# A ternary product turned first: two token tiles of a convolution moved from TensorE to ScalarE and VectorE

## The reference, cut to what matters

```python
h = bit_linear(x, w1)                 # x quantised per token, w1 ternary: 128 -> 512
h = depthwise_conv1d(h.transpose(0, 2, 1), conv_w, conv_b)   # 3 taps over tokens, padding 1
h = jax.nn.silu(h.transpose(0, 2, 1))
return bit_linear(h, w2)              # h quantised per token, w2 ternary: 512 -> 128
```

## Time and profile before

| what | value |
|---|---|
| median of 3 runs | 322.48 us (315.58 to 322.57) |
| the profiled execution | 317.07 us |
| its span, first to last instruction | 314.2 us |
| mean granted TensorE clock | 0.989 of full |

### The profile page before, as it was taken

One profiled execution on the slowest core, in us unless ns is written; L12 is line 12 of the kernel. 1 busy time (PEld: TensorE's weight loads), 2 busy tenths in 40 slices (PEclk: granted clock), 3 DMA queues, 4 the chain that ended last, 5 costly groups with the idle time before them and its releaser, 6 DMA issues.

```text
span 314.2 us, 6619 instructions
## 1 busy us (share of the span) xinstructions
PE 283.5 (90%) x2446; PEld 179.3 (57%) x2446; DVE 219.8 (70%) x481; ACT 195.1 (62%) x484; POOL 143.1 (46%) x252
## 2 busy tenths in 40 slices
PE   0899699899999989989899999999999988898893
PEld 0567556566666668656566677445445443355672
DVE  3777767896776642869566747988888689527834
ACT  2588467668777760886677820778867866534333
POOL 3523767794477762565465500086326208001320
PEclk9999889999999999999999999999999999999997
DMA  7920000000000000000000000000000000000001
GB/s 273 306 87 3 0 3 1 2 2 0 3 2 3 2 0 2 0 3 0 2 2 3 2 2 0 2 0 0 2 0 3 1 0 3 0 2 0 8 17 42
DMA packets 4834, 6.16 MB, mean 20 GB/s; under 512 B 834, under 2 KB 3650, under 8 KB 4676
## 3 DMA queue, kind: packets, MB, share of 16 engines
q1 hardware_dynamic: 4516, 5.42, 4.9%
q10 hardware_dynamic: 288, 0.33, 0.4%
HBM read 5.23 MB, written 0.52 MB: 18 GB/s over the span
## 4 chain that ended last, share of the span: by engine, by line
PE 67%; DVE 19%; ACT 7%; issue 5%; DMA 1%; POOL 1%; ACTq 0%; DVEq 0%; POOLq 0%
PE bank L721 58%; PE bank L794 5%; ACT pr L545 4%; DVE nmax L1343 3%; DVE qk L1388 3%; DVE xn L1287 1%; DMA x_sb<-in_x 1%; ACT pT L545 1%; DVE stats L1274 1%; PE bank L946 1%; PE bank L848 1%; DVE qs L1323 1%; PE bank L1014 1%; DVE xn L1669 1%; DVE pT L1359 1%
## 5 line engine op out<-in xcount | busy, mean ns | idle before, releaser
L645 ACT ACTIVATE pT<-bank 128x512 f32<-128x512 f32 (+1 forms) x80 | 44.5, 600 | 25.6 <-PE bank L721 25.1
L338 POOL TENSOR_SCALAR pr<-pr,pinv 128x256 f32<-128x256 f32 (+2 forms) x96 | 45.5, 492 | 29.7 <-DVE pinv L1351 29.6
L1388 DVE TENSOR_REDUCE qk<-bank 128x4 fp32r<-128x616 f32 x64 | 49.0, 796 | 13.6 <-PE bank L721 13.4
L545 ACT ACTIVATE pr<-bank,nmax 128x256 f32<-128x256 f32 (+2 forms) x96 | 44.4, 480 | 18.2 <-DVE nmax L1343 17.9
L721 PE MATMUL bank<-qs 64*128 64x256 f32 (+3 forms) x256 | 50.4, 477 | 4.1 <-ACT pr L545 3.8
L1343 DVE TENSOR_REDUCE nmax<-bank 128x2 f32<-128x512 f32 (+2 forms) x48 | 31.6, 687 | 14.5 <-PE bank L721 14.5
L721 PE MATMUL bank<-pT,v_sb 128*64 128x128 f32 (+2 forms) x320 | 38.4, 385 | 0.0
L338 POOL TENSOR_SCALAR pT<-pT,pinv 128x512 f32<-128x512 f32 x32 | 21.8, 693 | 23.9 <-DVE pinv L1351 23.9
L1359 DVE COPY pT<-bank 128x512 f32<-128x512 f32 (+1 forms) x32 | 30.4, 949 | 1.6 <-PE bank L794 1.5
L721 PEld LDWEIGHTS bank<-pT,v_sb 128*64 128x64 f32 x320 | 21.1, 136 | 14.1 <-issue 10.8
L721 PE MATMUL bank<-km,qk 64*128 64x308 f32 x128 | 27.7, 366 | 1.2 <-DVE qk L1388 1.1
(11 more groups left out here) (190 smaller groups left out, 578.9 us busy)
## 6 DMA issues: line engine op xcount, KB each, us to landing
pT<-in_wqk SPq DMA_DIRECT2D x1, 1024.0 KB, 6.3
cw_sb<-in_cw SPq DMA_DIRECT2D x1, 768.0 KB, 8.8
x_sb<-in_x SPq DMA_DIRECT2D x2, 256.0 KB, 5.5
pT<-in_wv SPq DMA_DIRECT2D x1, 512.0 KB, 7.1
wo_sb<-in_wo SPq DMA_DIRECT2D x1, 512.0 KB, 7.3
out<-x_sb SPq DMA_DIRECT2D x8, 64.0 KB, 1.5
onT<-in_consts ACTq DMA_DIRECT2D x1, 256.0 KB, 5.0
pT<-in_xwk SPq DMA_DIRECT2D x1, 256.0 KB, 7.5
```

Of the source, the lines that this page charges most:

```text
L338: nc.gpsimd.tensor_scalar(d, d, pinv[:, t, a:a + 1], 1.0, ALU.mult, ALU.mult).then_inc(norm_done, 1)
L545: nc.scalar.activation(prob[r][:, a, at:at + w], bank[:, SP[k % 2] + a, at:at + w], ACT.Exp, bias=nmax[:, t, a:a + 1], accum_out=psum[:, t ...
L645: nc.scalar.activation(px[rows, i, :], bank[rows, (ST0, ST1)[i % 2], :], ACT.Exp, scale=SD ** -0.5).then_inc(xexp_done, 1)
L1388: nc.vector.tensor_reduce(m, s_in, AX.X, ALU.max, negate=True).then_inc(round_done, 1)
```

## The change

For tokens 256 to 511 of batch 1 (tiles 6 and 7) the product with ternary w1 is made with hidden units on partitions: for each of 4 blocks of 128 hidden units (`hidden_block`) two products of 258 columns (128 channels in, w1 exact in fp32r in `w1_t`, the tokens' high and low part) into banks 1 and 2 in turn. ScalarE makes the centre tap with the bias (`centre_tap`, 128 x 256), VectorE adds the two outer taps (`outer_taps`, two scalar_tensor_tensor of 128 x 256) into `tap_y`, which lies in `qs`. After all four blocks TensorE transposes them back into the banks of tiles 6 and 7 (`turn_taps`, four transposes each), in place of `conv(6)` and `conv(7)`. The weights of the taps, per hidden unit, come by one more load (`taps`, 16 values per partition), and w1 stays ternary without its mean: GpSimd multiplies the mean into the taps and, in three more passes, into the convolution rows in step 8; it also copies w1 to `w1_t` at the start of `bias_rows`. The down products use two banks in turn (`DOWN_BANK`), so each waits for the `finish` two tiles back. In the tail ScalarE does both last silus ahead of `turned_hidden` 4 to 7.

```diff
@@ -45,6 +45,9 @@
 HALF = NT // 2
+TAPPED = (1,)
+NB = FH // P
+TAP_BANK = (1, 2)
 KEY_BANK = (0, 5)
@@ -54,6 +57,7 @@
 HIDDEN_BANK = (ST0, ST1)
+DOWN_BANK = (OB, PJ0)
 OUT_BANK = (ST1, ST0)
@@ -79,7 +83,7 @@
 def decoder_layer(nc, x, consts, wqk, wv, wo, ctxT, xwq, xbq, xwk, xbk, xwv, xbv, xwo, xbo, lam_in,
-                  w1, cw, cb, w2, out):
+                  w1, cw, cb, w2, taps, out):
     with ExitStack() as ctx:
@@ -148,6 +152,7 @@
         wc = cw_sb
+        tap_sb = sb("tap_sb", [P, NB, 4])
         wsum = sb("wsum", [P, 2])
@@ -202,6 +207,8 @@
         qf = onT[:, 6:8, :]
+        tap_y, = places(qs[:, :, :].rearrange("p a b -> p (a b)"), (NB, T // 2))
+        w1_t = xT_l[:, 0, :]
         qb0, qb1, qa = qk[:, 0, 0, 0:2, :], qk[:, 0, 0, 2:4, :], qk[:, 0, 1, 0:2, :]
@@ -251,6 +258,7 @@
         root_done = sem("root_done")
+        tap_ps, tap_act, tap_done, tap_scaled = sem_names("tap_ps", "tap_act", "tap_done", "tap_scaled")
         pool_chain, qb0_pool, scale_done, hdq_done, hq_last = sem_names(
@@ -273,7 +281,7 @@
             sp.dma_start(wo_sb[:, :, :], wo).then_inc(ld_o, 16)
-            for dst, src in ((w1_sb[:, :], w1), (w2_sb.rearrange("p (k c) -> p k c", c=C), w2),
+            for dst, src in ((tap_sb[:, :, :], taps), (w1_sb[:, :], w1), (w2_sb.rearrange("p (k c) -> p k c", c=C), w2),
                              (cw_sb[:, :, :].rearrange("p a d -> p (a d)"), cw.to_broadcast([P, 3 * FH]))):
@@ -379,6 +387,12 @@
                     pool.wait_ge(w1d_done, 1)
+                    nc.gpsimd.tensor_scalar(tap_sb[:, :, 0:3], tap_sb[:, :, 0:3], wmean[:, 0:1], 1.0, ALU.mult,
+                                            ALU.mult).then_inc(tap_scaled, 1)
+                    for k in range(3):
+                        link(nc.gpsimd.tensor_scalar(cw_sb[:, k, :], cw_sb[:, k, :], wmean[:, 0:1], 1.0, ALU.mult,
+                                                     ALU.mult))
+                    settle()
                     for k in range(3):
@@ -452,6 +466,8 @@
+                pool.wait_ge(xq_ps, NG)
+                nc.gpsimd.tensor_copy(w1_t, w1_sb[:, :]).then_inc(tap_scaled, 1)
                 pool.wait_ge(ld_cb, 16)
@@ -676,6 +692,16 @@
+            def centre_tap(b, k):
+                v = NB * TAPPED.index(b) + k
+                act.wait_ge(tap_ps, v + 1)
+                if v == 0:
+                    act.wait_ge(tap_scaled, 1)
+                if v == NB:
+                    act.wait_ge(conv_ps, NT)
+                nc.scalar.activation(tap_y[:, k, :], bank[:, TAP_BANK[k % 2], 1:T // 2 + 1], ACT.Identity,
+                                     bias=tap_sb[:, k, 3:4], scale=tap_sb[:, k, 1:2]).then_inc(tap_act, 1)
             whole, halves = slice(0, T), (slice(0, T // 2), slice(T // 2, T))
@@ -709,11 +735,18 @@
             turned_hidden(1)
-            for i in range(4, TT):
-                silu(i)
-                turned_hidden(i - 2)
-            turned_hidden(TT - 2)
-            turned_hidden(TT - 1)
+            silu(4)
+            centre_tap(1, 0)
+            centre_tap(1, 1)
+            turned_hidden(2)
+            centre_tap(1, 2)
+            centre_tap(1, 3)
+            silu(5)
+            turned_hidden(3)
+            silu(TT - 2)
+            silu(TT - 1)
+            for i in range(TT - 4, TT):
+                turned_hidden(i)
@@ -998,6 +1031,32 @@
+            def hidden_block(b, k):
+                v = NB * TAPPED.index(b) + k
+                if k == 0:
+                    pe.wait_ge(xdTl_done, 1 if b == 0 else 3)
+                if v == 0:
+                    pe.wait_ge(tap_scaled, 2)
+                if k < 2 and b == 0:
+                    pe.wait_ge(round_done, part_sums + 2)
+                elif k < 2:
+                    pe.wait_ge(silu_done, 3 + k)
+                else:
+                    pe.wait_ge(tap_done, v - 1)
+                o, w = bank[:, TAP_BANK[k % 2], 0:T // 2 + 2], w1_t[:, P * k:P * k + P]
+                mm(o, w, xdT_h[:, b, T // 2:T + 2], True, False)
+                mm(o, w, xdT_l[:, b, T // 2:T + 2], False, True).then_inc(tap_ps, 1)
+            def turn_taps(i):
+                pe.wait_ge(tap_done, NB * TAPPED.index(i // NT) + NB)
+                at = P * (i % NT - HALF)
+                for k in range(NB):
+                    last = nc.tensor.transpose(bank[:, CONV_BANK[i % 4], P * k:P * k + P], tap_y[:, k, at:at + P],
+                                               con[:, C_ID:C_ID + P])
+                last.then_inc(conv_ps, 1)
             def turn_hidden(i):
@@ -1019,10 +1078,12 @@
                     pe.wait_ge(xo_done, 2)
+                elif i == 1:
+                    pe.wait_ge(xdTl_done, 3)
                 else:
-                    pe.wait_ge(f_done, i)
+                    pe.wait_ge(f_done, i - 1)
                 for k in range(FH // P):
-                    last = mm(bank[:, OB, 0:C], hiT[:, i % 2, k * P:k * P + P], w2_q[:, k, :], k == 0,
+                    last = mm(bank[:, DOWN_BANK[i % 2], 0:C], hiT[:, i % 2, k * P:k * P + P], w2_q[:, k, :], k == 0,
                               k == FH // P - 1)
@@ -1247,11 +1308,19 @@
             turn_hidden(1)
-            conv(5)
-            for i in range(6, TT):
-                down(i - 5)
-                turn_hidden(i - 4)
-                conv(i)
+            conv(5, [0])
+            hidden_block(1, 0)
+            hidden_block(1, 1)
+            conv(5, [1])
+            down(1)
+            turn_hidden(2)
+            hidden_block(1, 2)
+            hidden_block(1, 3)
+            conv(5, [2])
+            down(2)
+            turn_hidden(3)
+            turn_taps(6)
+            turn_taps(7)
             for i in range(TT - 4, TT):
@@ -1308,8 +1377,7 @@
                 if k == 0:
-                    nc.vector.tensor_scalar(w1_sb[:, :], wq1, -1.0, wmean[:, 0:1], ALU.max,
-                                            ALU.mult).then_inc(w1d_done, 1)
+                    nc.vector.tensor_scalar(w1_sb[:, :], wq1, -1.0, None, ALU.max).then_inc(w1d_done, 1)
                     dve.wait_ge(w1d_done, 1)
@@ -1420,7 +1488,7 @@
             row_max(0, 1)
-            dve.wait_ge(ld_f, 48)
+            dve.wait_ge(ld_f, 64)
             for k, w in enumerate((w1_sb, w2_sb)):
@@ -1621,6 +1689,18 @@
+            def outer_taps(b, k):
+                v = NB * TAPPED.index(b) + k
+                dve.wait_ge(tap_act, v + 1)
+                if v == 0:
+                    dve.wait_ge(tap_scaled, 1)
+                ps = bank[:, TAP_BANK[k % 2], :]
+                link(nc.vector.scalar_tensor_tensor(tap_y[:, k, :], ps[:, 0:T // 2], tap_sb[:, k, 0:1], tap_y[:, k, :],
+                                                    ALU.mult, ALU.add))
+                settle()
+                nc.vector.scalar_tensor_tensor(tap_y[:, k, :], ps[:, 2:T // 2 + 2], tap_sb[:, k, 2:3], tap_y[:, k, :],
+                                               ALU.mult, ALU.add).then_inc(tap_done, 1)
             def half_root(h):
@@ -1703,7 +1783,7 @@
                 dve.wait_ge(f_ps, i + 1)
-                nc.vector.scalar_tensor_tensor(x_sb[:, i, :], bank[:, OB, 0:C], hdq[:, i:i + 1],
+                nc.vector.scalar_tensor_tensor(x_sb[:, i, :], bank[:, DOWN_BANK[i % 2], 0:C], hdq[:, i:i + 1],
                                                x_sb[:, i, :], ALU.mult, ALU.add).then_inc(f_done, 1)
@@ -1716,7 +1796,15 @@
             hidden_scale(3)
-            for i in range(4, TT):
+            outer_taps(1, 0)
+            outer_taps(1, 1)
+            finish(0)
+            hidden_scale(4)
+            outer_taps(1, 2)
+            outer_taps(1, 3)
+            finish(1)
+            hidden_scale(5)
+            for i in range(6, TT):
                 finish(i - 4)
@@ -1750,7 +1838,7 @@
 _NAMES = ["x", "consts", "wqk", "wv", "wo", "ctxT", "xwq", "xbq", "xwk", "xbk", "xwv", "xbv", "xwo", "xbo",
-          "lam_in", "w1", "cw", "cb", "w2"]
+          "lam_in", "w1", "cw", "cb", "w2", "taps"]
@@ -1815,6 +1903,8 @@
         "cb": g["L0_ffn_conv_b"][None, :],
+        "taps": np.concatenate([g["L0_ffn_conv_w"][:, 0, :], g["L0_ffn_conv_b"][:, None]], 1).reshape(
+            FH // P, P, 4).transpose(1, 0, 2),
         "w2": g["L0_ffn_w2"].T.reshape(FH // P, P, C).transpose(1, 0, 2),
```

## The result

The changed kernel takes 320.49 us (median of four, 320.4 to 320.72). Ratio to the kernel before 1.0124, 95% interval 1.0086 to 1.0162. The profiled execution takes 320.45 with a span of 318.4, against 317.07 and 314.2: the sum for it had said 315.1, so it is off by 5.3 us, and in direction.

A forecast was written before the change was run, and what follows sets the result against it. TensorE, busy 283.5 of 314.2 us, was taken as the bound, with the end waiting on one tile's path. Tail gains of 1.2 + 0.8 + 0.4, less 0.4 for the clock, gave 322.48 - 2.0 = 320.5 us, range 312.9 to 323.0.

The forecast's parts named there:

- the copy in `bias_rows`: GpSimd copy of 0.6 us before the xd transposes: no direct cost, taken as 0, with -1.0 to +0.6 kept.
- The tail: End of batch 1, tiles 4 to 7: gain 1.2 + 0.8 + 0.4 = 2.4 us, 2.0 after the clock.
- The thinnest cover: In the tail, the silu of tile 7 ends near 305.9 and VectorE wants it at 306.1: 0.2 us.
- The clock in the tail: Half speed may come before the last transposes as TensorE's work thins: 0.4 us taken off, up to 1.0.
- The two down banks: Kernel's end: last transposes start 0.05 behind the quantise, gain 0.8 us; `down(7)` 0.05 behind ScalarE, gain 0.4.
- POOL at n = 8: GpSimd's scale and three tap products ahead of `normalise(9, 0)`: 2.4 us under 8.5 us of cover, cost 0.
- the load: One more DMA issue on SP ahead of w1, w2 and cw: adds some 0.5 us, hidden, cost 0.
- Nothing is left of the tail: Rival for the tail: gain under 0.7 us through thin cover, clock and port order, giving 322; chance 0.14.
- slower, because DVE becomes a dearer bound: Rival for the tail: eight scalar_tensor_tensor at 0.73 us break even; with early half clock 323.2; chance 0.10.
- PE stays the bound: Rival for the tail: VectorE's pairs hidden, TensorE's whole saving back, 2.4 plus up to 1.0 us, giving 319; chance 0.06.
- The level of the runs: Rival for the whole kernel: runs mostly at the lower level, median 313.6 to 315.1 whatever the change does; chance 0.25.

The follow-up runs named there:

- filling the wait: Changed kernel with eight unused products of 512 columns in TensorE's queue ahead of its wait for the xd tiles: 314.17 us, ratio to the kernel before 0.9922.
- the new order: Changed kernel with bias_rows (with its copy) ahead of inverse_root(0, 5) in GpSimd's list: 311.73 us, ratio to the kernel before 0.9853.

## Why the prediction was wrong, step by step

**The step that failed is the copy in `bias_rows`.** The prediction had the two ends, "DVE ends 0.6 later" or "up to 1.0 earlier", and took 0. The upper end came: the order of the two operations was kept, 267.02 before 267.06, and TensorE's start moved by 0.55 more than the 0.09 ahead of it. But the step stopped at the delay. It had TensorE's wait of 1.30 in the earlier trace rows and a paragraph on the clock, and never put the two together: the clock was looked for in the tail only, where the work is thinned, and not where a wait that existed already got longer. The half clock there is no term of the sum: 6.1 us by the shifts, 6.3 by filling the wait. The sign that was to warn, a wait other than 1.3 by more than 0.6, was set too wide as well: 0.55 more was enough. The Trainium skill, "TensorE: Matmul & The Clock Gate", section "What's actually happening", which was weighed for the tail, applied here too: after little activity the engine is left at half rate, and full rate comes back only after it has been busy. The trace agrees in the order of things: the clock falls at 270.2, behind a stretch in which PE was busy 2.15 of 4 us, and is back at 283.9 behind 13.7 us in which it was busy throughout. Why the return takes that long here and 6.8 us in another execution, no run shows.

**The median came out as forecast, 320.49 for 320.5, by two errors that met, which is luck.** 322.48 was the median of three executions, two of which were at the upper level. The prediction called the level a property of the runs, "whatever the change does". It was the half clock, which the changed kernel had in all four executions (mean granted clock 0.972 or 0.973 in each, 0.989 in the profile of before): 322.5 less the tail's 2.5 and plus the 0.55 of the longer wait gives 320.5. Against the lower level, which the ratio uses, the same kernel is 1.2% slower. With the term put right the sum for the profiled execution is 317.07 + 0.1 + 0.55 + 6.1 - 2.5 = 321.3, for 320.45 measured; by spans 314.2 + 4.2 = 318.4, as measured. The 0.9 between the two sums lies outside the span (2.9 us in the profiled execution of before, 2.0 in this one).

**The tail was right.** Forecast 2.4 before the clock; the shifts give 2.53: 1.21 up to the last quantise (1.2 forecast), 0.82 to the last transposes (0.8), 0.32 to `down(7)` (0.4), and 0.18 that the forecast did not have (below). A scalar_tensor_tensor of 256 columns: 0.48 forecast, 0.475 and 0.484 measured. DVE's start at 298.0 on the old scale: 304.90 - 6.73 = 298.17. The last quantise ends at 307.5: 314.21 - 6.73 = 307.48. Between the last quantise and the last transposes, and between ScalarE and `down(7)`, lie 0.05 each, as forecast. A product of 258 columns was bounded by 0.13 and 0.26; the starts of the first four lie 0.12 apart. `centre_tap` was priced by the 0.372 of a plain cast and takes 0.560; the first outer taps start 0.17 later for it, and the later ones don't wait for it. The thinnest cover was thinner than forecast: the silu of tile 7 ends 0.03 us ahead of VectorE's row maximum (312.58 and 312.61), not 0.2.

**The clock in the tail.** 0.4 was taken off, with up to 1.0 in the range. Nothing came: the granted clock stays at 1.00 to about 317.9, behind the last down product. So thinning TensorE's work there did no harm, and nothing was to be taken off. It even gained: `down(7)` took 0.58 at half clock before and takes 0.40 now, the 0.18 above.

**The two down banks.** 0.8 + 0.4 = 1.2 was right for the end of the kernel, in the new order too, where one bank loses 1.1 behind the last quantise. But the second bank does more there: without it 4.4 us are lost by the profiles (5.0 by the medians, with the early stretch), 2.4 of them at `down(1)` and `down(2)`, which the prediction never looked at with one bank.

**POOL at n = 8 and the load** were right at cost 0. Of the changed kernel, for the earlier trace rows:

```profile
109.12 2.02 POOL L393 TENSOR_SCALAR cw_sb<-cw_sb,wmean 128x512 f32<-128x512 f32 x3
...
114.95 0.93 POOL L346 TENSOR_SCALAR pr<-pr,pinv 128x256 f32<-128x256 f32 x2
...
114.67 7.38 PE L754 MATMUL bank<-wo_sb,onT 128*128 128x128 f32 x64 [1.52 <-issue]
```

`normalise(9, 0)` is 2.47 us later (2.4 forecast), and the projection starts 0.09 later than before, as everything does between 45 and 266 us.

**The rivals.** "Nothing is left of the tail" and "slower, because DVE becomes a dearer bound" both named the wrong place: the tail kept all of its gain and the DVE operations cost what was forecast. The loss came with the order of GpSimd's and VectorE's operations, which was given 0.6 at the most. "PE stays the bound" fell with VectorE's chain without a wait. "The level of the runs" was the nearest: it saw the two levels, but took them for something outside the kernel.

## What to carry to other kernels

An engine's wait has a second price: where TensorE already waits over a microsecond, half a microsecond more can put its next 13.7 us at half clock (6 us lost here). So before an operation is added anywhere, look at whose wait grows by it, even where it is "hidden". And where the runs of a kernel fall on separate levels, look at the granted clock in a profile of an upper one before a difference is carried over to the median: the level can be a defect that an edit of two lines takes away, here by moving `bias_rows` to where GpSimd idles.

## What was unexpected in the hardware

- Near 270 us the half clock came in two lengths, about 6.8 and 13.7 us, and TensorE was busy all through both; elsewhere (near 38 us, and at 304.3 with one bank) it lasted 3.4. The same instructions after a wait of 1.3 us went either way: 18 of 71 executions of the kernel before above 318.5, 6 of 12 when run again, 5 of 12 for the changed kernel with a wait of 1.33, and none of 22 with the wait filled or of 10 with it gone. With 1.67 us nine of ten were above the lowest level, with 1.82 and 1.85 us all but one of eight. (The waits are those of the profiled executions.) What decides one execution is open.
- GpSimd operations on only 2 partitions (2x512, 1.27 us) hold a VectorE operation on 128 until they end: 0.90 instead of 0.16 us for a tensor_tensor of 4 columns, 1319 instead of 278 ns for a tensor_scalar of 128.
- A copy placed right behind the last of them is nearly as bad as one in front: TensorE waits 1.67 and 1.85 us (1.30 with none). The four xn operations take 2.27 us with the copy behind, 1.91 with none, 0.87 with GpSimd idle.
